# Issuing the first group's stack loads two units earlier on SyncE's queue

## The reference, cut to what matters

```
x = x + layernorm(attention0(layernorm(x)))   # queries and keys from normalized down-projections, 16 heads of 16
x = x + layernorm(ffn0(layernorm(x)))         # int8 weights 256 -> 1024 (gate, up) -> 256, silu
x = x + layernorm(attention1(layernorm(x)))   # plain qkv projection, 16 heads of 16, biases
x = x + layernorm(ffn1(layernorm(x)))
```

## Time and profile before

| what | value |
|---|---|
| median of three runs | 1266.66 us |
| the profiled execution | 1266.53 us, span 1264.8 us |
| PE busy | 1161.7 us (92%) |
| DVE busy | 1050.8 us (83%) |
| ACT busy | 721.5 us (57%) |
| POOL busy | 335.7 us (27%) |
| queue q1 (SP's DMAs) | 25376 packets, 41.95 MB, 11.7% of 16 engines |
| the chain that ended last | PE 70%, DVE 19%, ACT 3%, DMA 3%, POOL 3% |

### The profile page before, as it was taken

The page is one execution under the profiler, slowest core; times in us unless marked ns, Lnnn a source line. Parts: engine busy times, 40 slices in busy tenths (PEclk is TensorE's granted clock), DMA queues, the critical chain, the costliest instruction groups (busy, mean ns, idle before and its releaser), DMA issues.

```text
span 1264.8 us, 35512 instructions
## 1 busy us (share of the span) xinstructions
PE 1161.7 (92%) x14872; PEld 587.4 (46%) x14872; DVE 1050.8 (83%) x2746; ACT 721.5 (57%) x919; POOL 335.7 (27%) x561
## 2 busy tenths in 40 slices
PE   4779999999999998799978799999999999988996
PEld 4432344544444444466545224455444445354664
DVE  6869999999999863878863999999999988558776
ACT  2441377777677886234343407777777788833332
POOL 2331211122111233433443202111131112424443
PEclk9976799999999999899999659999999999998998
DMA  5364000211100000000026320021120000000001
GB/s 174 97 200 100 20 16 15 64 28 41 40 3 2 3 3 3 20 15 1 1 77 196 102 66 15 15 65 27 27 56 2 3 3 3 4 1 2 17 18 34
DMA packets 31600, 49.95 MB, mean 39 GB/s; under 512 B 7245, under 2 KB 24143, under 8 KB 31431
## 3 DMA queue, kind: packets, MB, share of 16 engines
q1 hardware_dynamic: 25376, 41.95, 11.7%
q0 software_dynamic: 5488, 5.34, 1.4%
q10 hardware_dynamic: 576, 0.39, 0.1%
HBM read 32.56 MB, written 14.68 MB: 37 GB/s over the span
## 4 chain that ended last, share of the span: by engine, by line
PE 70%; DVE 19%; ACT 3%; DMA 3%; POOL 3%; issue 2%; SPq 1%; ACTq 0%; POOLq 0%; DVEq 0%
PE ps L887 67%; DVE m_tile L780 6%; DVE ps L782 3%; DMA q_parts<-parts 2%; DVE region_p L640 1%; DVE stats L627 1%; ACT region_p L569 1%; POOL q_stack L455 1%; PE ps L1034 1%; DVE region_p L838 1%; DVE region_p L754 1%; PE ps L882 1%; DMA q_stack<-m_rows 1%; DMA causal<-in_causal 1%; DVE rem L681 1%
## 5 line engine op out<-in xcount | busy, mean ns | idle before, releaser
L569 ACT ACTIVATE region_p<-ps 128x1024 f32<-128x1024 f32 (+3 forms) x640 | 541.6, 894 | 247.1 <-PE ps L887 243.6
L780 DVE TENSOR_REDUCE m_tile<-ps 128x1 f32<-128x512 f32 x768 | 501.3, 685 | 27.9 <-PE ps L887 22.4
L887 PE MATMUL ps<-k_stack,q_stack 96*32 96x512 bf16 (+3 forms) x5120 | 435.8, 375 | 21.4 <-DVE m_tile L780 7.8
L887 PE MATMUL ps<-q_stack,k_stack 99*32 99x512 bf16 (+3 forms) x5120 | 351.2, 352 | 3.5 <-ACT region_p L569 2.2
L887 PE MATMUL ps<-region_p,v_all 128*17 128x512 f32 (+3 forms) x2560 | 293.1, 531 | 5.1 <-POOL region_p L460 4.9
L782 DVE CUSTOM_DVE_ANT_0 ps<-ps,causal 128x128 f32<-128x128 f32 (+3 forms) x512 | 248.6, 497 | 28.1 <-PE ps L887 26.7
L887 PEld LDWEIGHTS ps<-k_stack,q_stack 96*32 96x32 bf16 x5120 | 144.5, 97 | 255.4 <-DVE m_tile L780 106.5
L887 PEld LDWEIGHTS ps<-q_stack,k_stack 99*32 99x32 bf16 x5120 | 141.1, 98 | 153.1 <-issue 56.1
L460 POOL TENSOR_SCALAR_AFFINE_SELECT region_p<-region_p 128x512 f32<-128x512 f32 x128 | 81.4, 637 | 275.2 <-ACT region_p L569 269.6
L887 PE MATMUL ps<-region_a,w_ffn 128*128 128x512 f16 x512 | 124.3, 388 | 6.1 <-DVE region_a L672 5.2
L603 ACT ACTIVATE k_stack<-ps,cols 128x512 f32<-128x512 f32 x64 | 44.1, 688 | 128.3 <-PE ps L887 125.8
(11 more groups left out here) (93 smaller groups left out, 869.7 us busy)
## 6 DMA issues: line engine op xcount, KB each, us to landing
k_parts<-parts SPq DMA_DIRECT2D x16, 384.0 KB, 5.3
q_parts<-parts SPq DMA_DIRECT2D x16, 384.0 KB, 7.5
q_stack<-q_parts SPq DMA_DIRECT2D x32, 192.0 KB
k_stack<-k_parts SPq DMA_DIRECT2D x32, 192.0 KB
q_stack<-q_parts SPq DMA_DIRECT2D x32, 128.0 KB
k_stack<-k_parts SPq DMA_DIRECT2D x32, 128.0 KB
X<-in_x SPq DMA_DIRECT2D x4, 512.0 KB, 6.9
q_stack<-q_parts SPq DMA_DIRECT2D x32, 64.0 KB
```

The lines of the kernel that those rows point to most:

```text
L569: nc.scalar.activation(probs[:, o.j % SLOTS, 2 * o.hp:2 * o.hp + 2, o.off:CH], psT[:, o.k % 2, :, o.off:CH], ACT.Exp, scale=SCALE).then_in ...
L780: nc.vector.tensor_reduce(maximum, scores, AX.X, ALU.max).then_inc(s.ring_free, 1)
L887: return pe.matmul(o, a, b, start=first, stop=last)
```

## The change

It moves the place at which SP issues the stack loads of group 0. Nothing is added or removed.

```diff
                     for c in range(NCH):
-                        if u == min(CHUNK_UNITS[L] * (c + 1) + 3, NU - 1):
-                            parts_complete(CHUNK_UNITS[L] * (c + 1))
+                        if u == CHUNK_UNITS[L] * (c + 1) + 1:
+                            parts_complete(u - 1)
                             load_stacks(0, c)
```

## The result

The changed kernel takes 1277.25 us (median of four runs, 1276.89 to 1281.62), the kernel before 1267.04 us over its four. The ratio is 1.0085, with a 95% interval of 1.0067 to 1.0102: slower by 8.5 to 13 us. Forecast were 1274.6 us, a range of 1269 to 1279, and slower with a chance of 0.80. The profiled execution took 1275.28 us, its span is 1273.5 us.

A forecast was written before the change was run, and what follows sets the result against it. Both layers' projection stages were taken to hang on stores landing behind loads on SP's queue, holding up ACT. 1266.53 us plus 3.5 for layer 0 and 4.6 for layer 1 gave 1274.6 us, range 1269 to 1279.

The forecast's parts named there:

- Nobody waits for the stacks, and the stores behind them are waited for: Table of waits: no engine waits for stack loads; ACT waits four times, 21.2 us, for stores sharing their queue.
- Layer 1: one period less the head start, 4.6 us: Layer 1 projection: one more 8.57 us period (six loads, two stores), loads starting 4.0 us sooner; 4.6 us later.
- The upper bound of 5.5 us: Layer 1 projection: most time lost, allowing one of three periods to begin partly from a standstill.
- The busiest few engines set the period: Load queue: broadcast loads run on 3 and 2 engines, stores land when the last engine is through; 8.57 us per period.
- The queue does not run dry in layer 1: Layer 1, SP's new wait: the queue still holds the second group and two stores, 8.57 us of work.
- Layer 0: 3.5 us: Layer 0 projection: fifth value product 1.8 us later, plus 1.7 us from PE at half clock; 3.5 us later.
- the middle of the two bounds: Layer 0: unit 8's store lands at 76.9, between 75.4 (full queue) and 78.3 (standstill).
- The sum: Whole kernel: 1266.53 + 3.5 + 4.6 = 1274.6 us.
- Layer 0 even: Rival, layer 0: second group starts quickly, clock holds, no loss; only layer 1's 4.6 us remain, 1271.1 us; chance 0.17.
- hidden: Rival, both layers: queue has reserve, a group ahead costs little more than its head start; 1267.5 us; chance 0.11.
- dry queue: Rival, both layers: queue empties before each group, layer 1 19.7 us later, layer 0 5.8; 1292 us; chance 0.05.
- Faster: Rival, both layers: stores use engines the loads leave free, period under 4.0 us; 1259.8 us; chance 0.04.

The follow-up runs named there:

- the spread kernel: Against the kernel before, loads at their old places, each broadcast query load cut into DMAs of 16 rows, same bytes: 1255.70 us, ratio 0.9916.

## Why the prediction was right

- *Nobody waits for the stacks, and the stores behind them are waited for.* Right: ACT's waits nearly doubled, and no wait for the stacks vanished, as there was none.
- *Layer 1: one period less the head start, 4.6 us.* Measured 5.0, and 5.3 with layer 1 alone. The parts fit singly. The first loads start 4.4 us behind the first store (666.98 less 662.59), where it was 8.4: a head start of 4.0. The landing behind them comes 12.8 us later (12.6). The three periods are 8.99, 8.86 and 8.03 us, 25.9 in all (25.7). From the first loads to unit 15 it is 38.75 us (38.3). The upper bound of 5.5 us had no row for its last 0.9 us, and 5.0 lies under it.
- *The busiest few engines set the period.* Shown by the change of form: with the same bytes over all engines the 8.6 us periods and the waits are gone, and with them the effect of the place. But the prediction's row, a share of 0.19 over 680 to 684 us, is one half of a period only. The next row of the kernel before, the other half, has nearly all engines at work:

```profile
684.00:688.00 4.00, 4.00 (x17) 2.76 (x16) 0.00 (x0) 0.56 (x1) 0.00 (x0) 1.00 0.95 299
```

So about 4 of the 8.57 us pass with some three engines busy. No view names the single engines; their number is read from the share. The sum did not use the share, and stands. By the estimate from the Trainium skill, "DMA: Bandwidth & Descriptors", section "Specifications" (435 GB/s over 16 engines), layer 1 was to lose 3.7 us; the measured 5.0 is nearer to the rows' 4.6.

- *The queue does not run dry in layer 1.* Right, the periods stayed where they were.
- *Layer 0: 3.5 us.* Measured 3.9, and 4.6 with layer 0 alone. The first group's store landed 11.6 us behind its start (12.1 forecast), the second's 11.1 us (between 9.2 and 12.1; I took 10.7). From the first store, unit 13 came at 35.4 us; forecast were 77.0 - 41.6 = 35.4. That this agrees to 0.1 us is luck: the middle of the two bounds was taken without a row for it, and the 0.5 us by which the first landing came sooner and the 0.4 by which the second came later cancel. The clock fell as forecast (0.52 granted over 75.6 to 82.5 us), and for longer: PE's fifth and sixth product took 3.78 us, and unit 15's took 1.33 in place of 1.02.
- *The sum.* 8.1 us forecast, 8.9 in the two stages, 10.2 in the medians. The mechanism held, and the two terms were each about 10% short. Where the remaining 1.3 us lie is not shown; the interval, 8.5 to 13 us, holds the 8.9 of the stages, but not the 8.1 forecast.
- *The rivals.* "Layer 0 even" and "hidden" fell to the stages, "dry queue" to the periods. "Faster" needed stores that find free engines; the spread kernel shows this is what it takes, though the place then no longer matters.

What I had not taken apart in the prediction: in layer 0 the second group by itself loses, and in layer 1 the fourth. The first of layer 0 and the first three of layer 1 are nearly neutral.

## What to carry to other kernels

Before a load is issued earlier, look at what stands behind it on the same queue, and who waits for that. A prefetch that nobody waits for has little to win: here the best case was 0.6 us on a stage, the worst a loss of 6.1. Read the DMA share of the stretch: a low share with long landings is a sign that few engines carry the queue, and here it was the form of the transfers that had to be changed, not their place. Where a wait for a buffer passed the delay on, two more buffers hid it as well, with the loads at their old places; at the new ones the stages kept 3.5 and 1.5 us of it.

## What the runs showed of the hardware that was not expected

- With query loads written as broadcasts to 48 and 32 rows, the DMA share was 0.19, about 3 of 16 engines, for some 4 us of each 8.6; the same bytes in DMAs of 16 rows cut the median landing of the stores beside them from 8.4 to 3.3 us.
- Small DMAs on POOL's queue, 3 KB each, took up to 6.4 us from issue to landing while SP's loads kept the DMA engines busy (a share of 0.62 over the 10 us around them), 2.1 to 2.5 at a share of 0.15, and 1.6 to 1.8 at 0.04 or less.
- The granted clock can fall in one execution and not in another of the same program, far from the change. In the changed kernel PE has a stretch at half clock at the end of layer 0's attention that the kernel before has in neither profile: 0.53 was granted over 498.9 to 502.3 us, and 1.00 at the same place before. PE's timeline of the changed kernel there:

```profile
498.73 1.93 PE L887 MATMUL ps<-region_p,v_all 128*17 128x512 f32 x8
```

The kernel before has 1.03 us for the same eight passes in its timeline:

```profile
496.15 1.03 PE L887 MATMUL ps<-region_p,v_all 128*17 128x512 f32 x8
```

The stretch from the last scores of layer 0 to layer 1's first store takes 177.1 us with it and 174.9 without. The kernel in which only layer 1's fourth group is moved shows the same (177.1), though its program is the old one up to there, so the moved loads are not needed for it. The kernel with layer 0 alone moved, up to there the changed kernel's program, took 175.4. The stretch accounts for the 2.0 us between the stages in the profile after. Whether it falls more often in the changed kernel's unprofiled runs, and so makes part of the 1.3 us, stays open; so does why the time before the first store varies between 40.4 and 44.0 us, and the attention of layer 0 between 399.4 and 401.2 us in the changed kernel and the one with layer 0 alone moved.
